# A gated recurrence on one core: gate Z summed over three groups instead of four, and gate R's last products in another order

## The reference

```
ys = cond * C**-0.5
d  = rsqrt((ys*ys) @ (W*W) + 1e-8)
x1 = x + ((x * ys) @ W) * d

for every step t, H starting from cond:
    Z  = sigmoid(x1[t] @ Wxz.T + bxz + H @ Whz.T + bhz)
    R  = sigmoid(x1[t] @ Wxr.T + bxr + H @ Whr.T + bhr)
    Ht = tanh(x1[t] @ Wxh.T + bxh + (R*H) @ Whh.T + bhh)
    H  = Z*H + (1-Z)*Ht
    Y[t] = H @ Whq.T + bhq
out = x1 + Y
```

## Time and profile before

| | before |
|---|---|
| median of 3 runs | 636.63 us |
| the profiled execution, its own time | 637.65 us |
| its span (first to last instruction) | 635.9 us |
| mean granted clock of TensorE over the span | 0.527 |
| PE busy | 624.7 us (98%) |
| DVE busy | 465.4 us (73%) |
| ACT busy | 279.5 us (44%) |

### The profile page before, as it was taken

One profiled execution on the slowest core, in us unless ns is written; L12 is line 12 of the kernel. 1 busy time (PEld: TensorE's weight loads), 2 busy tenths in 40 slices (PEclk: granted clock), 3 DMA queues, 4 the chain that ended last, 5 costly groups with the idle time before them and its releaser, 6 DMA issues.

```text
span 635.9 us, 40091 instructions
## 1 busy us (share of the span) xinstructions
PE 624.7 (98%) x16890; PEld 566.6 (89%) x16890; DVE 465.4 (73%) x3794; ACT 279.5 (44%) x2119; POOL 4.5 (1%) x11
## 2 busy tenths in 40 slices
PE   8999999999999999999999999999999999999987
PEld 3589999999999999999999999999999999999976
DVE  3888777776777777777777777777677777767776
ACT  2244444444444444444444444444444444444443
POOL 0200000000000000000000000000000000000000
PEclk9955555555555555555555555555555555555555
DMA  7000000000000000000000000000000000000000
GB/s 265 2 4 4 5 12 5 3 13 4 13 4 13 4 5 12 5 12 5 11 6 4 13 4 13 4 5 12 5 12 5 12 5 4 12 4 13 4 12 12
DMA packets 7176, 8.87 MB, mean 14 GB/s; under 512 B 1618, under 2 KB 5458, under 8 KB 6996
## 3 DMA queue, kind: packets, MB, share of 16 engines
q1 hardware_dynamic: 6416, 6.03, 3.0%
q10 hardware_dynamic: 580, 0.28, 0.2%
HBM read 4.21 MB, written 2.10 MB: 10 GB/s over the span
## 4 chain that ended last, share of the span: by engine, by line
PE 93%; DVE 4%; ACT 1%; DMA 1%; issue 1%; DVEq 0%
PE chunk_bank L691 53%; PE z_rec_bank L691 13%; PE chunk_bank L668 12%; PE z_bank L668 6%; PE y_bank L653 6%; PE chunk_bank L700 2%; DMA x<-x_cm 1%; PE chunk_bank L605 1%; DVE lin L404 1%; DVE r_hidden L538 1%; DVE hidden L584 1%; DVE r_hidden L542 0%; DVE r_hidden L546 0%; ACT scan_mul L343 0%; DVE xs L397 0%
## 5 line engine op out<-in xcount | busy, mean ns | idle before, releaser
L691 PE MATMUL chunk_bank<-r_hidden,w_part 128*128 128x8 bf16 x6144 | 206.3, 169 | 0.2
L691 PEld LDWEIGHTS chunk_bank<-r_hidden,w_part 128*128 128x128 bf16 x6144 | 184.7, 105 | 19.5 <-issue 0.6
L343 ACT ACTIVATE scan_mul<-z_pre 128x16 f32<-128x16 f32 x256 | 57.2, 224 | 196.8 <-DVE z_pre L550 196.8
L691 PEld LDWEIGHTS chunk_bank<-hidden,w_part 128*128 128x128 bf16 x3072 | 102.8, 104 | 30.8 <-DVE hidden L584 6.0
L691 PE MATMUL chunk_bank<-hidden,w_part 128*128 128x8 bf16 x3072 | 125.2, 173 | 4.4 <-DVE hidden L584 3.9
L691 PE MATMUL z_rec_bank<-hidden_parts,w_part 128*128 128x24 bf16 x3072 | 121.6, 181 | 0.1
L691 PE MATMUL chunk_bank<-hidden_parts,w_part 128*128 128x8 bf16 x3072 | 117.8, 168 | 0.0
L538 DVE TENSOR_TENSOR r_hidden<-r_bank,hidden 128x8 f32<-128x8 f32 x256 | 42.6, 166 | 97.0 <-ACT r_bank L341 95.3
L691 PEld LDWEIGHTS z_rec_bank<-hidden_parts,w_part 128*128 128x128 bf16 x3072 | 103.3, 104 | 0.2 <-DVE z_rec_bank L486 0.2
L691 PEld LDWEIGHTS chunk_bank<-hidden_parts,w_part 128*128 128x128 bf16 x3072 | 101.5, 104 | 0.0
L584 DVE TENSOR_TENSOR_SCAN hidden<-scan_mul,r_bank 128x24 f32<-128x24 f32 x256 | 52.0, 203 | 58.0 <-ACT r_bank L346 52.2
(11 more groups left out here) (92 smaller groups left out, 801.5 us busy)
## 6 DMA issues: line engine op xcount, KB each, us to landing
x<-x_cm SPq DMA_DIRECT2D x4, 512.0 KB, 8.1
out_cm<-result SPq DMA_DIRECT2D x15, 128.0 KB, 2.2
w_rec<-w_rec_cm SPq DMA_DIRECT2D x1, 768.0 KB, 8.5
w_in<-w_in_cm SPq DMA_DIRECT2D x1, 768.0 KB, 10.2
w_mod<-w_mod_cm ACTq DMA_DIRECT2D x1, 256.0 KB, 5.7
w_out<-w_out_cm SPq DMA_DIRECT2D x1, 256.0 KB, 10.6
out_cm<-result SPq DMA_DIRECT2D x1, 64.0 KB, 2.5
out_cm<-result SPq DMA_DIRECT2D x2, 32.0 KB, 1.9
```

Of the source, the lines that this page charges most:

```text
L343: nc.scalar.activation(scan_mul[:, :, 2::3], z_pre[:, :, :], ACT.Sigmoid, scale=-1.0)
L691: return nc.tensor.matmul(cols, w_part[wp][:, gate, k, m * P:(m + 1) * P], moving, start=first, stop=True, skip_group_check=True)
```

## The change

Gate Z keeps three groups instead of four. ScalarE writes the input share into group 0 and zeros into groups 1 and 2, by two ACTIVATEs instead of one, and PE's products are added to all three; none of them starts the bank anew. So that every addition finds the bank in the adding state, one product of zeros with `start=True` goes over the 48 columns once, before the loop, behind `d_sq_ready`. The reduction on DVE reads 2 x 8 x 3 values instead of 2 x 8 x 4. In `gate_products`, for gate R alone, `products(1, 0, 2, 1)` moves from ahead of the wait for `rest2[1]` to behind the product that this wait is for. For gate G the order stays.

```diff
-    Z_GROUPS = PARTS + 1
+    Z_GROUPS = PARTS
...
             def seed_z(parity, j):
-                nc.scalar.activation(
-                    z_rec_bank[:, 0:KC * Z_GROUPS * B].rearrange("p (m g b) -> p m g b", m=KC, g=Z_GROUPS)[:, :, PARTS, :],
-                    z_in[:, parity, :, j, :], ACT.Copy).then_inc(z_seeded, 1)
+                groups = z_rec_bank[:, 0:KC * Z_GROUPS * B].rearrange("p (m g b) -> p m g b", m=KC, g=Z_GROUPS)
+                nc.scalar.activation(groups[:, :, 0, :], z_in[:, parity, :, j, :], ACT.Copy)
+                nc.scalar.activation(groups[:, :, 1:Z_GROUPS, :], zeros[:, 0:KC * (Z_GROUPS - 1) * B].rearrange(
+                    "p (m g b) -> p m g b", m=KC, g=Z_GROUPS - 1), ACT.Copy).then_inc(z_seeded, 1)
...
+            act.wait_ge(zeros_ready, 1)
             act.wait_ge(wide_ready, 1)
...
             for m in range(KC):
-                at = (m * Z_GROUPS + PARTS) * B
+                at = m * Z_GROUPS * B
                 seed = nc.vector.tensor_scalar(z_rec_bank[:, at:at + B], z_bank[:, m * BC:m * BC + B],
...
             lin_tiles(1)
             lin_tiles(2)
+            pe.wait_ge(d_sq_ready, 1)
+            nc.tensor.matmul(z_rec_bank[:, 0:KC * Z_GROUPS * B], zeros[:, 0:P], zeros[:, 0:KC * Z_GROUPS * B],
+                             start=True, stop=True, skip_group_check=True)
...
                 pe.wait_ge(rest2[0], t + 1)
                 products(0, 0, 1, 2)
-                products(1, 0, 2, 1)
+                if gate == G:
+                    products(1, 0, 2, 1)
                 pe.wait_ge(rest2[1], t + 1)
                 products(0, 1, 1, 2).then_inc(done[0], 1)
+                if gate == R:
+                    products(1, 0, 2, 1)
                 products(1, 1, 2, 1)
                 products(1, 0, 1, 2)
                 products(1, 1, 1, 2).then_inc(done[1], 1)
...
                             mm = rec(z_rec_bank[:, m * Z_GROUPS * B:(m * Z_GROUPS + PARTS) * B], Z, m, k, wp,
-                                     h_parts(k, before, 0, PARTS), m == 0 and k == 0 and wp == 0)
+                                     h_parts(k, before, 0, PARTS))
```

## The result

The changed kernel takes 647.88 us, the median of 4 runs (647.66 to 649.49), beside 636.69 for the kernel before: a ratio of 1.018 (95% interval 1.0162 to 1.0198), **11.2 us slower**. I had forecast 646.0, which is 9.4 slower; the time lies in my range of 639.5 to 650.0. The profiled execution took 649.49 us with a span of 647.7; it is the longest of the four.

A forecast was written before the change was run, and what follows sets the result against it. The prediction took a loop over three engines, not PE's throughput, as the bound. It summed 240 x (0.05 - 0.01) - 16 x 0.01 = +9.4 us onto the median 636.63, forecasting 646.0, range 639.5 to 650.0.

The forecast's parts named there:

- PE now stops for 0.04 us in R ... I take 0.05: R's wait for H's third part: awaited product, now number 18, comes before its data; R's last product ends 0.05 later.
- That is late next: the gain is 0.01 us: Gate Z's reduction, about 0.015 us shorter; G's awaited product holds the first Tanh, so only 0.01 a step is gained.
- theory C: From the experiments, not the prediction: two loops, through output chunk 0 (with the reduction) and chunk 1; the longer sets the step.
- PE is on it only through R's last product and G's twentieth: The loop over three engines that sets the step: PE enters it only at these two products.
- ScalarE's second seed: Gate Z's extra ACTIVATE on ScalarE, about 0.2 us with some 0.11 start-to-start: covered before the scan's feeds, cost nothing.
- Accumulating instead of starting: Gate Z's 12 products on PE, added onto a seed, keep 24 columns and run at 0.027: nothing either way.
- The 16 steps with fp32 products: Steps where R's loads are held, 0.38 us instead of 0.33: no stop at the awaited product, only the 0.01 gain.
- Rival 1: R's moved products pay if H's third part is usable 0.04 us earlier: faster, 634.0 us; chance 0.08.
- Its worse half: The faster rival's further case: G's end also follows its earlier start, 256 x 0.06, giving 621 us.
- Rival 2: R's weight load is let through ahead of the wait, matmuls stop 0.02 less: 641.4 us; chance 0.07.
- rival 3: Gate Z gives nothing, or its seed gets in the way: 0.05 to 0.06 a step, 648.6 to 652; chance 0.05.
- Rival 4: R's and gate Z's parts cancel to under 0.005 a step; the stop would have to be 0.01; chance 0.03.

The follow-up runs named there:

- experiment 5: Changed kernel, but R's awaited product 18 takes H's second part again and the wait for the third stands two products later: 633.14 us, ratio 0.9942.
- experiment 7: Changed kernel, but with one product moved behind R's awaited one instead of two: 640.83 us, ratio 1.0069.
- experiment 2: Kernel before with R's new order alone, gate Z left at four groups: 647.64 us, ratio 1.018.
- Experiment 3: Kernel before plus one ACTIVATE of 32 columns of zeros a step, into columns nobody reads: 636.31 us, ratio 1.0003.

## Why the prediction was right, and where it wasn't

**Direction and main term: right.** The two moved products had covered the lateness of H's third part. Step "PE now stops for 0.04 us in R ... I take 0.05": R's order alone lengthens the second half of R from 0.40 to 0.44 and the step from 2.354 to 2.400, and experiment 5 shows that without that wait the same order costs nothing.

**The term that was mis-sized is gate Z's gain**, "That is late next: the gain is 0.01 us", which I subtracted in all 256 steps. In this change it was worth nothing: 2.400 with it and without it. I had looked for what is late next in the first Tanh only, where G's product 20 was 0.01 behind. But with the stop in R the loop through chunk 1 is the longest, and the reduction isn't in it. The earlier first scan lets R start earlier, and R then waits for the third part that much longer: its second half takes 0.46 us with gate Z's part and 0.44 without. Without the subtraction my sum is 240 x 0.05 = 12 us for the measured 11.2. Put by theory C: the new order makes the chunk-1 loop 2.347 + 2 x 0.027 = 2.400, which is 0.046 over the old step.

**"PE is on it only through R's last product and G's twentieth"** was half of the truth. G's last product sets the second Tanh, the second scan's end and H's third part. I took H's third part to keep its distance from R's first load, and so the second scan to follow the first, since the printed starts do (0.12 apart in every kernel here). That this gave the right stop is in part luck. With two products moved that account gives 2.394 us a step and theory C 2.400, and my range holds both. With one product moved they give 2.362 and 2.373, and experiment 7 measured 2.374.

One thing stays between the two accounts. In experiment 2 the second scan's row is at its shortest, 177 ns and steady (176 to 178), so there it may well follow the first scan as closely as its Tanh. Then the path through the reduction is as long in that kernel as the loop through chunk 1, 2.400 us, and shortening the reduction alone gains nothing.

**ScalarE's second seed: right, free.** Experiment 3 has an ACTIVATE of the same 32 columns of zeros in the old kernel at 636.31 for 636.34. **Accumulating instead of starting: right, free**, since gate Z alone runs at 2.347.

**The 16 steps with fp32 products: no stop, right.** Their reductions in the changed kernel, and R's loads 13 to 24 in one of these steps, 0.40 us as before:

```profile
L552 DVE TENSOR_REDUCE z_pre<-z_rec_bank x15: 200/200/201, 40.3 to 74.0; 128x16 f32<-128x48 f32 x15
```
```profile
55.97 0.40 PEld L693 LDWEIGHTS chunk_bank<-hidden_parts,w_part 128*128 128x128 bf16 x12
```

33.7 / 14 = 2.407 us a step, and in the kernel before the 15 reductions from 39.8 to 73.5 give 2.407 too. The 0.01 gain that I gave them doesn't show.

**The rivals.** Rival 1 (faster) didn't come, but it named its own condition rightly: with the third part out of the way the kernel is faster (2.341 a step, experiment 5). Its worse half, that G follows its start (621 us), is refuted by experiment 5, where G starts early and ends no earlier. Rival 2 (half the stop is swallowed, 641.4) is refuted by experiment 2: the whole stop arrives. The rule of the Trainium skill on pulling weight loads ahead ("TensorE: Matmul & The Clock Gate", the table ahead of Part 1) doesn't shorten a wait here; each awaited load stands 0.05 us behind its releaser. Of rival 3 the first half holds, gate Z gives nothing in this change, but the step grew by 0.046 and not by its 0.05 to 0.06; the second half, a seed that gets in the way, is refuted by experiment 3. Rival 4 (the parts cancel to under 0.005 a step) is refuted by the 0.046.

## What to carry to other kernels

Products that stand ahead of a wait are its cover: before one moves behind the wait, compare the awaited data's arrival with the slot that the awaited instruction would then have. If the data was just in time before, as here, price the move at one slot for each product that moves, less what the loop has to spare. Where two output chunks alternate, write out the loop of each through all engines. A gain counts only in the loop that is longest after the change, not before it, and two parts of one change are not added unless they lie in the same loop.

## What the runs showed of the hardware that I had not expected

The printed start of a VectorE instruction doesn't show how closely it follows what it waits for. The second scan starts 0.12 us behind the first in all ten kernels, while its median length goes from 177 to 203 ns and its end stays 0.39 to 0.40 us behind the second Tanh's start. Where a row grows with unchanged work, look for what its end follows, and read the slack from ends. Why the end and not the start moves with the Tanh, no run here shows: the start stands behind the Tanh's own end in each timeline above (302.42 for 302.20 + 0.16 in the kernel before).
